# Shared experts of a routed feed-forward layer: tiles 4 to 15 taken in three groups of four, with the weights of gate and up stationary and 512 tokens moving, and the gate mixing on GpSimd

## What is computed

```
xn = layernorm(x1)                                   # per token, 512 values
logits = xn @ router_w.T                             # 8 experts, top 1
out = x1 + glu(xn, shared_gate.T, shared_up.T, shared_down.T)
         + sigmoid(top logit) * glu(xn, w1[e], v1[e], w2[e])
glu(x, wg, wu, wd) = (silu(x @ wg) * (x @ wu)) @ wd  # all 512 x 512, float32
```

## Time and profile before

| | |
|---|---|
| median of three runs | 413.68 us |
| the profiled execution: its span, first to last instruction | 411.6 us |
| TensorE matmul busy | 385.1 us (94%) |
| VectorE busy | 258.2 us (63%) |
| ScalarE busy | 161.2 us (39%) |
| GpSimd busy | 134.6 us (33%) |
| DMA | 55.96 MB, mean 136 GB/s |

### The profile page before, as it was taken

The page is one execution under the profiler, slowest core; times in us unless marked ns, Lnnn a source line. Parts: engine busy times, 40 slices in busy tenths (PEclk is TensorE's granted clock), DMA queues, the critical chain, the costliest instruction groups (busy, mean ns, idle before and its releaser), DMA issues.

```text
span 411.6 us, 6789 instructions
## 1 busy us (share of the span) xinstructions
PE 385.1 (94%) x1982; PEld 303.8 (74%) x1986; DVE 258.2 (63%) x475; ACT 161.2 (39%) x274; POOL 134.6 (33%) x186
## 2 busy tenths in 40 slices
PE   5875659999999999999999999999999999999994
PEld 2442238888888788887888888888888888888883
DVE  6997876555857865656875557547375744676322
ACT  3996852223344324211116245153254515354110
POOL 7787811000100100005030245425535442446201
PEclk9998999999999999999999999999999999999999
DMA  8900502011201561140041469726546773752210
GB/s 321 397 2 0 204 1 78 27 51 60 90 30 53 187 247 53 53 153 27 32 133 41 128 217 323 282 98 256 204 134 219 294 258 118 262 182 71 86 37 30
DMA packets 14763, 55.96 MB, mean 136 GB/s; under 512 B 2575, under 2 KB 2575, under 8 KB 11280
## 3 DMA queue, kind: packets, MB, share of 16 engines
q1 hardware_dynamic: 9936, 40.93, 28.0%
q0 software_dynamic: 4800, 14.69, 10.0%
HBM read 43.02 MB, written 13.63 MB: 138 GB/s over the span
## 4 chain that ended last, share of the span: by engine, by line
PE 81%; DVE 7%; ACT 5%; issue 3%; POOL 2%; DMA 1%; DVEq 0%; POOLq 0%; ACTq 0%
PE GU L1255 47%; PE yb L1255 22%; PE th L1247 4%; PE tx L1240 4%; ACT tiles L534 2%; PE th L1284 2%; DVE search_junk L806 1%; ACT scratch L545 1%; ACT scratch L549 1%; DMA x_sb<-x_tok 1%; PE mb L1255 1%; DVE x_sb L864 1%; DVE tiles L862 1%; DVE bn_parts L871 1%; PE mb L1233 0%
## 5 line engine op out<-in xcount | busy, mean ns | idle before, releaser
L1255 PE MATMUL GU<-w_parts,xT 128*128 (+1 forms) x864 | 213.6, 395 | 0.0
L1255 PEld LDWEIGHTS GU<-w_parts,xT 128*128 128x128 f32 x864 | 158.3, 188 | 31.4
L1255 PE MATMUL yb<-w_parts,hT 128*128 (+1 forms) x420 | 102.6, 392 | 0.0
L1255 PEld LDWEIGHTS yb<-w_parts,hT 128*128 128x128 f32 x420 | 77.8, 188 | 15.7
L605 ACT ACTIVATE hT<-th 128x512 fp32r<-128x512 f32 x36 | 21.6, 599 | 170.8 <-PE th L1247 170.8
L472 POOL DMA_INDIRECT out<-x_sb,scatidx x20 | 37.6, 1879 | 92.5 <-DVE x_sb L1098 85.6
L922 DVE TENSOR_TENSOR w_parts<-w_raw,w_parts 128x2048 f32 (+1 forms) x24 | 54.9, 2288 | 7.4 <-issue 7.2
L907 DVE TENSOR_TENSOR hidden<-hidden,GU 128x512 f32<-128x512 f32 x36 | 24.8, 688 | 40.2 <-PE GU L1255 40.1
L522 ACT ACTIVATE w_parts<-w_raw 128x2048 f32 (+1 forms) x24 | 45.2, 1910 | 4.2 <-issue 3.9
L446 POOL TENSOR_TENSOR x_rstd<-x_mv,eps 128x1 f32<-128x1 f32 x16 | 3.0, 190 | 113.4 <-DVE x_mv L874 113.4
L901 DVE TENSOR_TENSOR hT<-th,hT 128x512 fp32r<-128x512 f32 x36 | 24.8, 689 | 23.9 <-ACT hT L605 23.6
(11 more groups left out here) (233 smaller groups left out, 339.8 us busy)
## 6 DMA issues: line engine op xcount, KB each, us to landing
w_raw<-weights SPq DMA_DIRECT2D x27, 1024.0 KB, 5.3
x_sb<-x_tok SPq DMA_DIRECT2D x8, 512.0 KB, 6.5
xn_d<-tiles SPq DMA_DIRECT2D x16, 256.0 KB, 2.0
z_d<-x_sb SPq DMA_DIRECT2D x16, 256.0 KB, 2.0
tiles<-xn_d,tokidx POOLq DMA_INDIRECT x20, 4.7
x_sb<-z_d,tokidx POOLq DMA_INDIRECT x20, 5.5
out<-x_sb,scatidx POOLq DMA_INDIRECT x20, 6.8
conv<-conv_par SPq DMA_DIRECT2D x1, 10.0 KB, 9.0
```

The source lines that it names most:

```text
L1255: last = pe.matmul(dst, left[:, lp, kc, :], wset(q, k, wp, kc), start=(i == 0), stop=(i == 3 * KC - 1))
```

## The change

Tiles 0 to 3 stay as they were, one by one. Tiles 4 to 15 go in three groups of four. Of each group the transposed, split tokens lie side by side (512 of them) in the place of set 1's weights (`quad_x`: the down matrix for groups 1 and 3, the gate matrix for group 2). A gate or up product is now made by chunks of 128 hidden channels: the weights' 128 columns are stationary and the 512 tokens move (`chunk_product`), so h comes out with channels on partitions and is split without a transpose (`chunk_hi` on ScalarE, `chunk_lo` on VectorE, both out of `hidden`). The down product stays per tile (`tile_down`), with the banks `yb` and `th` in turn. The logits of a group are 8 matmuls of 512 columns into `mb` (`route_quad`).

For tiles 4 to 15 GpSimd multiplies by the gates and adds to x, ahead of each tile's `rstd_tile`. All gates are stored, those of images 6 and 7 in `scratch`. Since set 1's place is taken, its split comes late: HI by ScalarE after chunk 11's up product (gate, up) and after chunk 15's (down), LO of gate and up by GpSimd behind the sigmoid's powers, LO of down by VectorE behind tile 13's add. SP's loads and stores are in an order written out by hand; the load of set 1's down matrix waits for tile 11's multiplication on GpSimd. Cut to its core:

```diff
-PREPARED = ((3,), (4,), (5,), (6, 7), (8,), (9,), (10, 11), (12,), (13,), (14,), (15,))
-SPLIT_AFTER = (4, 5, 8)
+SINGLE = 4
+QUAD = 4
...
+        def quad_x(quad):
+            return w_parts[:, 1, GATE if quad == 2 else DOWN, :, :, :]
...
+        def shared_y(t):
+            return th if t >= SINGLE and t % 2 else yb
...
             for t in range(NT):
+                if t >= SINGLE:
+                    mix_tile(t, t % RING, t // 2)
                 rstd_tile(t, t % RING)
...
+            for k in (GATE, UP):
+                pool.wait_ge(whi, k + 1)
+                for kc in range(KC):
+                    low = pool.tensor_tensor(w_parts[:, 1, k, LO, kc, :], w_raw[:, k, kc, :],
+                                             w_parts[:, 1, k, HI, kc, :].bitcast(F32), ALU.subtract)
+                low.then_inc(wlo, 1)
...
+            mix_tile(3, 3, 1)
+            measure(3)
+            measure(4)
+            norm(3)
+            h_lo(0, 0)
+            gated(1, 1)
+            turn_lo(3)
...
+            norm(7)
+            add_shared(2)
+            measure(8)
+            turn_lo(7)
...
             choose()
+            add_shared(8)
+            add_shared(9)
+            add_shared(10)
             slots_of_tokens()
+            add_shared(11)
+            gated(12, 0)
+            chunk_lo(12)
             place()
+            gated(13, 1)
+            chunk_lo(13)
             fields()
+            gated(14, 0)
+            chunk_lo(14)
             slot_tables()
...
+            def chunk_product(m, which):
+                dst, i = gu(m % 2, which), 0
+                x, rows = quad_x(m // QUAD), slice(m % QUAD * P, (m % QUAD + 1) * P)
+                for kc in range(KC):
+                    for wp, xp in ((HI, HI), (LO, HI), (HI, LO)):
+                        last = pe.matmul(dst, wset(0, which, wp, kc)[:, rows], x[:, xp, kc, :], start=(i == 0), stop=(i == 3 * KC - 1))
+                        i += 1
+                return last
+            def chunk_gate(m):
+                if m % QUAD == 0:
+                    pe.wait_ge(xlo, m + QUAD)
+                if m > SINGLE + 1:
+                    pe.wait_ge(silu, m - 1)
+                chunk_product(m, GATE).then_inc(g_done, 1)
...
+            def quad_down(quad, after_second, after_third):
+                t = quad * QUAD
+                tile_down(t, range(0, 3))
+                tile_down(t + 1, range(0, 3))
+                tile_down(t, range(3, KC))
+                tile_down(t + 1, range(3, KC))
+                after_second()
+                tile_down(t + 2, range(0, KC))
+                after_third()
+                tile_down(t + 3, range(0, KC))
...
+            prepare(7)
+            spread_gate(7)
+            chunk_gate(4)
+            transpose_h(3, 1)
+            pe.wait_ge(y_used, 3)
+            turn_logits(0)
+            chunk_up(4)
+            prepare(8)
+            pe.wait_ge(logits_used, 1)
+            down_product(3, 1, 0, 0)
+            route_quad(1)
+            chunk_gate(5)
+            turn_logits(1)
+            chunk_up(5)
+            prepare(9)
+            for m, t in ((6, 10), (7, 11)):
+                chunk_gate(m)
+                chunk_up(m)
+                prepare(t)
+            quad_down(1, lambda: None, lambda: prepare(12))
+            route_quad(2)
...
+            quad_down(2, lambda: None, rank)
+            for m in (12, 13):
+                chunk_gate(m)
+                chunk_up(m)
+            chunk_gate(14)
+            chunk_up(14)
             fill_slots()
+            chunk_gate(15)
+            chunk_up(15)
...
+            quad_down(3, lambda: None, first_block)
             gate_product(NT, 0, 0, 1, 3)
             pe.wait_ge(xg_in[1], 16)
             transpose_x(NT + 1, xg[:, 1, :])
             up_product(NT, 0, 0, 1, 3)
-            down_product(n + 4, 1, 0, 0)
+            pe.wait_ge(y_used, NT)
```

More of the change, by code:

```diff
@@ L627, in _, with turn_hi, again @@
                                ACT.Copy).then_inc(xhi_half if half == 0 else xhi, 1)
-            x_hi(1, 1)
+            def turn_hi(t):
+                x_hi(t, x_parts(t, HI))
+            def again(t):
+                norm_a(t, t % RING)
+            turn_hi(1)
             silu_gate(0, 0)
+            again(4)
             keep_logits(0)
-            x_hi(2, 2)
+            turn_hi(2)
             keep_logits(1)
[L633 to L655, removed]
@@ new lines, in _ @@
+            again(9)
+            store_gate(7, mb)
+            h_hi(3, 1)
+            silu_gate(4, 0)
+            turn_hi(8)
+            chunk_hi(4)
+            again(10)
+            again(11)
+            keep_quad(1)
+            for m, t in ((5, 9), (6, 10), (7, 11)):
+                silu_gate(m, m % 2)
+                turn_hi(t)
+                chunk_hi(m)
+                again(t + 3)
+            turn_hi(12)
+            again(15)
+            keep_quad(2)
+            for m, t in ((8, 13), (9, 14), (10, 15)):
+                silu_gate(m, m % 2)
+                turn_hi(t)
+                chunk_hi(m)
@@ L658, in _ @@
+            for k in (GATE, UP):
+                x_hi(NT + k, xT[:, k, HI, :, :])
                 act.wait_ge(w_in[k], 16 * 3)
@@ L934, in _, with norm @@
             gate_tile(2, 2, 1)
-            x_lo(1, 1)
-            norm_tile(2, 2)
-            gated(0, 0)
[L938 to L956, removed]
+            def norm(t):
+                norm_tile(t, t % RING)
@@ new lines, in _ @@
+            measure(10)
+            gated(5, 1)
+            turn_lo(9)
+            chunk_lo(5)
+            take_logits(1)
+            norm(10)
+            measure(11)
+            gated(6, 0)
+            turn_lo(10)
+            chunk_lo(6)
+            norm(11)
+            measure(12)
+            gated(7, 1)
+            turn_lo(11)
+            chunk_lo(7)
+            norm(12)
+            measure(13)
+            add_shared(4)
+            add_shared(5)
+            norm(13)
+            turn_lo(12)
@@ L959, in carve @@
+            add_shared(6)
+            measure(14)
+            add_shared(7)
+            gated(8, 0)
+            turn_lo(13)
+            chunk_lo(8)
+            take_logits(2)
+            norm(14)
+            measure(15)
+            gated(9, 1)
+            turn_lo(14)
+            chunk_lo(9)
+            norm(15)
+            gated(10, 0)
+            turn_lo(15)
+            chunk_lo(10)
+            gated(11, 1)
+            chunk_lo(11)
             def carve(space, at, *widths):
```

378 lines of the change are left out of this document (249 added, 129 removed).

## The result

The changed kernel takes **416.74 us** (median of 4 runs, 415.32 to 416.99) against 413.62 us before (413.54 to 413.94): a ratio of 1.0063, 95% interval 1.0050 to 1.0076. It is slower by 3.1 us, where 1.6 us faster was forecast, and the time lies above the range.

The account below looks back on a forecast made before the run. TensorE was taken as the bound: 8.5 us saved less 6.5 of waits gave 2.0 faster; with 0.4 added for collisions, 413.7 became 412.1 us, range 409.6 to 415.0.

Parts of the forecast that it names:

- What leaves TensorE's queue: TensorE's queue: h transposes, narrow routes and small logit groups go, three wide routes come; 8.5 us saved.
- Tile 3: Ahead of tile 3's x transposes: VectorE measures tile 4 first, which waits for GpSimd's mixing; 2.3 us lost.
- Chunk 4: Ahead of the first chunk of the first group: TensorE waits for tile 7's final form; 1.5 us lost.
- The third tile's bank: Each group's third tile reuses the first's bank and waits for VectorE's add; 1.2 us lost over three groups.
- The slots: Ahead of the matmuls filling the slots: VectorE's fields and selection outlast two covering product groups; 1.5 us lost.
- The first rival: GpSimd's split passes and VectorE's slot steps collide: 1.9 us at slots, 0.3 near tile 7; 413.9 us, chance 0.20.
- The third rival: TensorE's clock falls behind the gap at tile 3, 1.7 us lost; 413.8 us, chance 0.08.
- The second rival: GpSimd's passes exceed 1.27 us, at tile 3 and the splits ahead of the slots; +3.8, 417.5 us, chance 0.14.
- The fourth: Waits are covered better than thought, at the slots and chunk 4 above all; -4.6, 409.1 us, chance 0.13.

Follow-up runs that it names:

- 409.50 us: Changed kernel with only three orders changed: tiles 4 and 8 measured later, slots filled behind chunk 15's gate group; 409.50 us, ratio 0.9888.

## Why the prediction was wrong

Step by step, as the prediction put them.

- **What leaves TensorE's queue**, 8.5 us: 6.5 by the ledger, 7.1 without the bank wait hidden in its row for down, so 1.4 too much. The jobs themselves came out well: the ledger has h transposes -4.8, routes -0.6 and turned logits -0.8, where the bare terms (12 times 0.41; 12 times 0.47 against 3 times 1.82; 0.5) were -4.9, -0.2 and -0.5. What did not come in full is the 0.12 to 0.13 that each of 24 groups was to be shorter for not starting behind such a job: that is 2.8 us in the sum, while gate and up together gave 1.6. The x transposes and spread gates took 0.5 more, and down 0.2 more beside the bank wait; why is not isolated.
- **Tile 3**, 2.3 us: 2.32, by the walk told.
- **Chunk 4**, 1.5: 1.00. **The third tile's bank**, 1.2: 0.93 over the three quads, by the walk told.
- **The slots**, 1.5: 1.41 in both runs without passes beside the steps. The walk was right.
- **The first rival, taken at 0.4 of its 2.2**: this is the first step that failed. Seven waits were the rival's own count, and seven came; at the slots they cost 1.58 of the 1.9 it named. The argument against, that "by the code only three of the thirteen surely read two SBUF operands", was no bound: steps with one SBUF input, TENSOR_SCALAR and CAST, waited as well, four of the seven. The Trainium skill (SBUF — State Buffer, "Who interferes with whom") lists casts and `tensor_scalar` among the instructions that can take the shared port pair, where their operands meet its conditions, and says that a `tensor_reduce` on this chip does not contend. The trace agrees step by step: 1.21 for L1196 and 0.83 for L1195, 0.29 for both reductions.
- **The third rival, the clock**: the step that cost most. It had a chance of 0.08, one place and 1.7 us; it came in two places and took 3.4. "Against: there the engine had done little before, here it is full" fell: the clock was 1.00 under full load ahead of both holes and 0.62 and 0.67 behind them. At the slots the runs show the hole as the cause; behind tile 3 the fall is measured (1.7 of the 3.4), but two other executions with that hole kept 1.00, so what decided it there stays open. The hole at the slots, lengthened by the collision to 2.99, was not even looked at as a place. With the hole at 1.41 there was no fall, so collision and clock come together there, where the rivals were told as alternatives.
- **The second rival** fell: GpSimd's passes over a tile average 1.29 to 1.32 us. **The fourth** fell with the holes.

The sum: 1.4 less saved, 1.1 more at the slots (2.99 against 1.5 and 0.4), 3.4 of clock, less 0.8 at chunk 4 and the bank, make 5.1. For the stage -1.6 was forecast (2.0 less 0.4) and +3.5 measured, which is the same 5.1. The change was a good one in a bad order, as 409.50 us shows with every collision left in place.

## What to carry over

A wait put into a bound engine's queue can be priced twice: by its length, and by what the engine's clock does behind it; here holes of two to three microseconds were worth hiding by a reordering. When work moves to GpSimd, list what VectorE does in just that stretch, one-input steps and tiny ones included: a step of 24 elements can wait as long as the whole series of passes. Where such a collision can't be moved to a quiet place, put products over it; that beat each attempt to remove it.

## What the runs showed of the hardware that was not expected

- A step of VectorE can wait for a whole series of GpSimd passes, not for one: 5.72 us for a step of 0.35, and 5.01 for one of 0.16, beside four passes of 1.23 to 1.25. At the slots, though, steps and passes took turns. Why one and the other is open; no run was made for it.
- The granted clock fell right out of full load behind holes of 2.32, 2.82, 2.99, 3.00, 3.03, 3.73 and 5.62 us (0.62, 0.74, 0.67, 0.57, 0.59, 0.63 and 0.50 in a stretch of 4 us at or behind the hole), and to 0.79 over two holes of 1.43 and 1.77 with 1.7 us of work between them. It did not fall behind a single 1.00, 1.41 or 1.43. Behind the 2.35 at tile 3 it stayed at 1.00 in two other executions (with the splits on VectorE, and with the splits behind the slots), so near that length it is not the same each time. Those two had a low clock shortly ahead of the first product, the kernel after had not; whether that matters is not shown.
- Reductions, and steps with one operand in PSUM (L1186 and L1192, 0.29 each), were not delayed by the passes in the kernel after.
